# Attention in a four-layer fp32 kernel: VectorE's product of the output one step later, behind the next group's first row maxima

## The reference, cut to what matters

```
q = l2norm(q) * q_scale
k = l2norm(k) * k_scale
sim = jnp.einsum('bhid,bjd->bhij', q, k) * SCALE
...
sim = sim + attn_bias
...
sim = jnp.where(causal, neg, sim)
...
attn = jax.nn.softmax(sim, axis=-1)
out = jnp.einsum('bhij,bjd->bhid', attn, v)
```

## Time and profile before

| | |
|---|---|
| median of three runs | 2767.54 us |
| the profiled execution, whole | 2769.7 us |
| its span, first to last instruction | 2767.7 us |
| mean granted TensorE clock | 0.893 |
| TensorE busy over the span | 2141.7 us, 77% |
| VectorE busy | 1081.8 us, 39% |
| ScalarE busy | 961.8 us, 35% |
| GpSimd busy | 675.4 us, 24% |

### The profile page before, as it was taken

One profiled execution on the slowest core, in us unless ns is written; L12 is line 12 of the kernel. 1 busy time (PEld: TensorE's weight loads), 2 busy tenths in 40 slices (PEclk: granted clock), 3 DMA queues, 4 the chain that ended last, 5 costly groups with the idle time before them and its releaser, 6 DMA issues. The chain is left out here.

```text
span 2767.7 us, 45649 instructions
## 1 busy us (share of the span) xinstructions
PE 2141.7 (77%) x15902; PEld 1473.8 (53%) x15903; DVE 1081.8 (39%) x3083; ACT 961.8 (35%) x2531; POOL 675.4 (24%) x1062
## 2 busy tenths in 40 slices
PE   2988888877898887299947843966798888639991
PEld 1555665644665556176644632853465665516660
DVE  5367663265666612000024322016467662201112
ACT  0266662045676610012101310213567661002220
POOL 2011111166111111600054144026611111140005
PEclk8999999998999997599958975988899999769995
DMA  3011105000000001124131341430000000421113
GB/s 84 1 59 40 40 21 179 33 19 16 17 17 16 3 18 63 51 91 136 54 101 69 95 148 59 152 122 10 16 17 17 10 10 18 161 99 46 45 36 99
DMA packets 105962, 158.26 MB, mean 57 GB/s; under 512 B 14586, under 2 KB 74896, under 8 KB 105772
## 3 DMA queue, kind: packets, MB, share of 16 engines
q1 hardware_dynamic: 89196, 112.77, 12.8%
q0 software_dynamic: 16576, 42.99, 4.6%
HBM read 120.53 MB, written 47.27 MB: 61 GB/s over the span
## 5 line engine op out<-in xcount | busy, mean ns | idle before, releaser
L806 ACT ACTIVATE att_pr<-all_h,att_nmax 128x128 f32<-128x128 f32 (+3 forms) x768 | 421.9, 552 | 167.9 <-DVE att_nmax L764 167.7
L764 DVE CUSTOM_DVE_ANT_0 all_h<-att_s_ps,att_bias,mem_nsn 128x128 f32<-128x128 f32 (+3 forms) x768 | 382.0, 542 | 119.8 <-PE att_s_ps L848 98.9
L878 PE MATMUL att_o_ps<-att_pt,mem_v 128*64 128x128 f32 x3840 | 293.1, 282 | 1.7 <-DVE mem_qt L781 0.2
L859 PEld LDWEIGHTS att_pt_ps<-all_ident,att_pr 64*128 64x128 f32 x3840 | 163.3, 139 | 234.8 <-DVE att_pt L771 167.7
L848 PE MATMUL att_s_ps<-mem_kt,mem_qt 64*128 64x512 f32 (+3 forms) x1536 | 285.7, 447 | 0.0
L859 PE MATMUL att_pt_ps<-all_ident,att_pr 64*128 64x64 f32 x3840 | 192.3, 228 | 91.5 <-DVE att_pt L771 84.4
L878 PEld LDWEIGHTS att_o_ps<-att_pt,mem_v 128*64 128x64 f32 x3840 | 202.8, 136 | 38.2 <-issue 18.2
L998 PE MATMUL out_y_ps<-out_wo,mem_qt 128*128 128x256 f32 x768 | 178.3, 385 | 8.9 <-ACT out_pn_t L946 8.9
L771 DVE COPY att_pt<-att_pt_ps 128x256 f32<-128x256 f32 (+3 forms) x240 | 177.5, 739 | 0.8 <-PE att_pt_ps L859 0.6
L1445 PE MATMUL exp_f_h_ps<-exp_f_xs_t,cw_f_w 128*128 128x512 f32 (+1 forms) x512 | 171.6, 494 | 1.5 <-DVE exp_f_xs_t L1482 1.5
L1457 PE MATMUL exp_f_y_ps<-cw_f_w,exp_f_hid 128*128 128x256 f32 x768 | 168.4, 379 | 0.0
(11 more groups left out here) (310 smaller groups left out, 3069.9 us busy)
## 6 DMA issues: line engine op xcount, KB each, us to landing
cw_f_w<-in_L_ffn_w_dram SPq DMA_DIRECT2D x16, 1024.0 KB, 7.1
cw_f_w<-in_L_ffn_W_dram SPq DMA_DIRECT2D x16, 1024.0 KB, 8.3
band<-rev SPq DMA_DIRECT2D x2, 4096.0 KB, 27.8
att_bias<-band SPq DMA_DIRECT2D x32, 256.0 KB, 2.9
til_c_xs<-sorted SPq DMA_DIRECT2D x40, 128.0 KB, 2.1
expert<-til_c_ys POOLq DMA_DIRECT2D x40, 128.0 KB, 2.0
til_f_xs<-sorted SPq DMA_DIRECT2D x40, 128.0 KB, 2.0
expert<-til_f_ys POOLq DMA_DIRECT2D x40, 128.0 KB, 2.0
```

The costliest lines, as they stand in the source:

```text
L764: nc.vector.tensor_tensor_reduce(sc[p % 4][:, hh, 0:n], s_ps[p % 2][hh][:, 0:n], bias_ap(i, q, hh), -1.0, c.nsn[:, b, q, h:h + 1], ALU.add ...
L806: nc.scalar.activation(pr[p % 3][:, hh, 0:n], sc[p % 4][:, hh, 0:n], ACT.Exp, scale=-1.0, bias=nmax[:, b, q, h:h + 1], accum_out=rsum[:, b ...
L859: last = nc.tensor.transpose(pt_ps[:, n, (q + 1) * hh + kb, :], pr[p % 3][d, hh, P * kb:P * (kb + 1)], c.ident[d, d])
L878: last = nc.tensor.matmul(o_ps[DH * hh:DH * (hh + 1), b, :], c.v[:, QT * b + kb, :], pt[p % 4][:, P * ((q + 1) * hh + kb):P * ((q + 1) * h ...
```

## The change

VectorE's `put_out` is written one step later and at another place in the step. Before, it was the last thing in loop 4G+2: behind `largest(4G+3)` and `take_pt(4G+1)`, and ahead of `largest(4G+4)`. Now it is in loop 4G+3: behind `largest(4G+4)`, the first maxima of the next group, and ahead of `take_pt(4G+2)`, which VectorE has only where q = 0. No instruction is added or removed, and no other engine's order changes.

```diff
             for p in range(NP + 4):
                 if p + 1 < NP:
                     largest(p + 1)
+                if p % B == 3 and p > B:
+                    put_out(p // B - 1)
                 if 1 <= p <= NP and taken_by_vector(p - 1):
                     take_pt(p - 1)
                 if p % B == 0 and p:
                     invert(p // B - 1)
-                if p % B == 2 and p > B:
-                    put_out(p // B - 1)
             dve.wait_ge(out_ready, NG)
```

## The result

The changed kernel took 2701.42 us in the median of four runs (2698.71 to 2704.0), the kernel before 2768.2 us in the same comparison: ratio 0.9758, 95% interval 0.9741 to 0.9775. The forecast was 2704, with a range of 2688 to 2736. The profiled executions took 2702.2 and 2769.7 us, 67.5 us apart; the sum had said 63.7.

What follows compares the result with a forecast made beforehand. TensorE was taken to bound the attentions, idling for VectorE's copy queued behind the waiting product. Four passage savings, 21.2 + 10.8 + 20.4 + 11.3 = 63.7 us, took 2767.5 to 2704; range 2688 to 2736, likeliest case 2692 to 2722.

Steps and rivals of the forecast that it cites:

- the sum: Savings of the four passage kinds over three attentions: 21.2 + 10.8 + 20.4 + 11.3 = 63.7 us.
- What bounds: In the attentions TensorE leads; 84.4 us of its idle time ends with VectorE's P^T copy, queued behind the waiting product.
- copy waits: TensorE's idle time before transposes, ended by VectorE's P^T copy; forecast to fall from 84.4 to 15 to 25 us.
- 0 to 3: Passage from a group with key tile q = 0 to one with q = 3; 1.01 us saved, 21 times.
- 3 to 1: Passage from a q = 3 group to a q = 1 group; 0.45 us saved, TensorE's whole wait, 24 times.
- 1 to 2: Passage from a q = 1 group to a q = 2 group; 0.85 us saved, 24 times.
- 2 to 0: Passage from a q = 2 group to a q = 0 group; 0.54 us saved, 21 times.
- the replay: The prediction's retiming of each passage in the new order, using start-to-start distances from the old kernel's profile rows.
- Half of it: Rival: ScalarE's exponentials become the bound at the longer passages; 32 us saved, 2736 us; chance 0.12.
- No change: Rival: the single P^T buffer causes the bubble, so time returns before the same transpose; 2767 us; chance 0.04.
- Slower: Rival: the late product frees the output buffer late and holds up the values; 35 us lost, 2803; chance 0.04.
- What would show it: Expected profile signs: idle time before the product falls from 194.4 to about 40 us, copy waits to 15 to 25.

## Why the prediction was right, point by point

- *What bounds.* Right. TensorE's idle time in the attentions was VectorE's copy, and the same stretch in which VectorE stood in front of the product. The copy waits fell by 59.0 us.
- *0 to 3: 1.01 us.* Right in two attentions, 0.91 in attention 0. The product is late by the maxima that do not fit, and this makes nobody wait for it, as predicted.
- *3 to 1: 0.45 us.* The one term that was mis-sized. It is 0.61, and the next transpose gains another 0.06 (1.92 us behind this one instead of 1.98). The step that failed is "TensorE's scores end at 312.50, later. So the transpose starts at 312.50". The end of a row of matmuls is modelled, and in these traces the next one does not wait for it. Above, the scores end at 301.52 + 0.60 = 302.12 and the transpose has started at 301.95, 0.17 us sooner. The kernel before shows the same, so this could have been read before: its scores of the earlier trace rows end at 320.05, and the transpose behind them, shown with the profile after, starts at 319.89. With 0.17 us less the replay would have had the transpose at 312.33, a gain of 0.62. Where the copy is the later one, as in the other three terms, this does not enter. 24 x 0.22 = 5.3 us.
- *1 to 2 and 2 to 0: 0.85 and 0.54 us.* Right, 0.84 and 0.54, but for 1.19 at 1 to 2 in the second attention, which comes below.
- *The sum.* First to last product, the attentions became shorter by 22.2, 25.8 and 23.1 us, together 71.1 (the first attention reaches to 444 us in the kernel before, not to 430). By the distances between transposes this is 20.5 us at 0 to 3, 16.2 at 3 to 1, 23.0 at 1 to 2 and 11.4 at 2 to 0, where the sum had 21.2, 10.8, 20.4 and 11.3, together 63.7. So the sum was 7.4 us too low for the attentions: 5.3 by the mis-sized term, 2.8 by the second attention, less 0.7 in attention 0. Outside them 3.6 us were lost, so 67.5 in total. These 3.6 are 1.4 us ahead of the first product, 0.3 and 0.1 between the attentions, and 1.8 behind the last. Nothing of the change touches these parts, and the other profiles show that they scatter: the span beside the attentions is 1916.4 us before, 1920.0 after, 1920.0 in the changed kernel run again and 1916.0 with the product behind the copy. In the changed kernel run again the first product starts 1.8 us sooner than in the first profile, and the end comes 2.9 us later behind the last. That the time came out within 3 us of the forecast therefore owes something to luck: 7.4 us that the sum lacked stand against 3.6 outside the attentions that have nothing to do with it.
- *The second attention's 25.8.* It had 2.9 us more to lose, which the prediction did not see. The range of the products' starts, of before, second and third attention:

```profile
L781 DVE TENSOR_TENSOR mem_qt<-att_o_ps,att_rb_sb x32: 690/691/693, 693.2 to 978.9; 128x512 f32<-128x512 f32 x32
L781 DVE TENSOR_TENSOR mem_qt<-att_o_ps,att_rb_sb x32: 690/691/692, 2012.1 to 2294.9; 128x512 f32<-128x512 f32 x32
```

  They are 285.7 and 282.8 us long, with the same work. The difference is in one place of each head pair, at 1 to 2; this is the timeline of the second attention of before:

```profile
739.13 1.09 PE L878 MATMUL att_o_ps<-att_pt,mem_v 128*64 128x128 f32 x16
...
740.69 0.69 DVE L781 TENSOR_TENSOR mem_qt<-att_o_ps,att_rb_sb 128x512 f32<-128x512 f32 x1 [2.97 <-PE att_o_ps L878]
```

  The product starts 0.47 us after the end of the values (740.22). The run with only the passage 0 to 3 changed, which keeps this place as it was, has the same delay in the same attention. At the same place of the first attention the product starts at 319.25, 0.12 us after the end of these values:

```profile
318.04 1.09 PE L878 MATMUL att_o_ps<-att_pt,mem_v 128*64 128x128 f32 x16
```

  In the kernel after, the three attentions are 260.6, 259.9 and 259.7 us long: it is gone. What delays a waiting product by 0.35 us in one attention and not in another stays open.
- *The rivals.* Half of it: no, ScalarE's waits for maxima fell from 167.7 to 97.7 us. No change, by the single P^T buffer: no, though no run had a second one; the rule of the Trainium skill (Perfetto Trace Analysis, Optimization Strategy) names buffers as a possible cause of a bubble that repeats, and here the same bubble went with the order of one queue, the buffer as before. Slower, by the late release of the output buffer: not here, but real one loop further on.
- *What would show it.* The idle time ahead of the product was forecast at about 40 us and is 40.8, but two errors cancel in this. The passages leave 28.6 us where 34 were forecast, above all at 2 to 0 (0.67 us each instead of 0.81) and 1 to 2 (3.7 us in all instead of 6.7). The six products without a next group leave 12.9 us and not a few: 1.35 and 2.96 in each attention, as in the kernel before. (Together this is 41.5 us, of which 40.8 end with the values.) The copy waits were forecast at 15 to 25 and are 25.4; what is left is 0.45 at each 0 to 3 of attention 0, 0.35 at those of the other two, and 0.56 at a copy of a q = 3 group that has no product in front, here from the timeline of the third attention of the kernel after:

```profile
1998.62 0.71 PE L859 MATMUL att_pt_ps<-all_ident,att_pr 64*128 64x64 f32 x16 [0.56 <-DVE att_pt L771]
```

## What to carry to other kernels

When an in-order engine stands in front of one instruction, look at what is queued behind it and whether its inputs are ready already. Work that fits under the wait can be put in front. The gain is at most that work: at 2 to 0 it was all 0.54 us of it. It is less where the moved instruction itself comes late (1.01 us of 1.34 at 0 to 3), where the work behind it must wait for inputs of its own (0.84 of 1.08 at 1 to 2), and where the delayed engine's own work is the later one (0.67 of 0.81 at 3 to 1). The idle time of the delayed engine is no bound: at 1 to 2 it was 0.70 and the gain 0.84. Count then how late the moved instruction may come before it holds up its own readers: here it had one loop, and not two. Within a queue that is itself the chain, another order gave nothing; an instruction given to an idle engine did.

## What the runs showed that was not expected

At 3 to 1, where no wait stands between, a transpose starts 0.17 us before the modelled end of the scores ahead of it. The kernel before has the same distance, and a sum that takes such an end as the earliest start is too pessimistic by that much at each place. And a product that had been waiting for a semaphore started 0.47 us after its releaser's end at one place of one attention, and 0.12 at the same place of the others, each of the eight times that it came round.
